# Second layer of a fused attention and mixture-of-experts kernel: biases of the sorted tiles summed by TensorE, row transfers held to planned steps, norms spread over more steps

## Time and profile before

| what | value |
|---|---|
| median of 3 runs | 2873.52 us (2866.96 to 2877.98) |
| profiled execution, its own time | 2869.59 us |
| its span | 2867.9 us |
| VectorE busy | 2243.4 us, 78% |
| ScalarE busy | 1236.5 us, 43% |
| TensorE matmuls busy | 1195.6 us, 42% |
| GpSimd busy | 289.9 us, 10% |
| first `B` of batches 0, 1, 2, 3 | 1572.9, 1798.4, 2093.3, 2416.2 us |
| last `B` of batch 3, end | 2694.6, 2867.9 us |

### The profile page before, as it was taken

How to read it: one execution, slowest core, us unless ns; L and a number is a source line. 1 busy time by engine, 2 the same in 40 slices (tenths; PEclk the granted TensorE clock), 3 DMA queues, 4 the chain that set the end, 5 groups by cost and what they waited for, 6 DMA issues and landing times. The chain is left out here.

```text
span 2867.9 us, 37860 instructions
## 1 busy us (share of the span) xinstructions
PE 1195.6 (42%) x7272; PEld 536.4 (19%) x7272; DVE 2243.4 (78%) x15187; ACT 1236.5 (43%) x3176; POOL 289.9 (10%) x425
## 2 busy tenths in 40 slices
PE   3010100101010000101004887788876887778697
PEld 1000000000000000000001111223421342133365
DVE  5999999999999999999975899856657665864133
ACT  1333333333333333333360556656655664567542
POOL 0000000000000000000010020031023212201211
PEclk9999999999999999999996899979987998889898
DMA  5000000000000000000034020103110212001100
GB/s 135 1 1 1 1 1 1 1 1 1 1 1 1 1 1 1 1 1 1 1 68 103 1 67 20 24 22 89 26 44 23 74 37 52 18 17 30 33 1 23
DMA packets 79603, 66.11 MB, mean 23 GB/s; under 512 B 8126, under 2 KB 64232, under 8 KB 79368
## 3 DMA queue, kind: packets, MB, share of 16 engines
q1 hardware_dynamic: 76296, 57.40, 8.3%
q0 software_dynamic: 3072, 6.30, 0.7%
HBM read 34.77 MB, written 28.57 MB: 22 GB/s over the span
## 5 line engine op out<-in xcount | busy, mean ns | idle before, releaser
L1309 DVE TENSOR_REDUCE nm_half<-pair 128x2 f32<-128x1024 f32 x512 | 611.7, 1219 | 224.1 <-PE pair L1557 188.6
L203 ACT ACTIVATE ex<-row,nmax 128x65 f32<-128x65 f32 x960 | 336.0, 350 | 923.8 <-DVE nmax L305 837.3
L1196 ACT ACTIVATE pt<-pair 128x1024 f32<-128x1024 f32 x512 | 510.2, 1027 | 389.2 <-PE pair L1567 357.9
L263 DVE SCALAR_TENSOR_TENSOR junk<-ex,tab 128x65 f32<-128x65 f32 x2850 | 620.0, 218 | 1.4 <-issue 0.4
L366 PE MATMUL p_s<-tab,bdg 128*128 128x32 f32 x120 | 31.9, 406 | 829.2 <-DVE tab L268 829.2
L1533 PE MATMUL p_o<-pt,va 128*9 128x512 f32 x2048 | 299.2, 659 | 9.7 <-ACT pt L1196 8.3
L268 DVE TENSOR_TENSOR tab<-raw,rz 128x1 f32<-128x1 f32 (+1 forms) x1890 | 284.8, 151 | 3.2 <-issue 1.1
L297 DVE SCALAR_TENSOR_TENSOR junk<-ex,rz,row 128x65 f32<-128x65 f32 x930 | 265.4, 285 | 3.0 <-issue 2.7
L1557 PE MATMUL pair<-ks,qs 48*128 48x512 bf16 x1024 | 212.8, 420 | 123.3 <-ACT pt L1196 75.4
L1567 PE MATMUL pair<-qs,ks 50*128 50x512 bf16 x1024 | 209.7, 414 | 62.4 <-DVE nm_half L1309 30.4
L263 DVE DVE_READ_ACCUMULATOR junk<-ex,tab 128x1 f32 x2850 | 233.8, 82 | 0.3
(11 more groups left out here) (254 smaller groups left out, 1908.1 us busy)
## 6 DMA issues: line engine op xcount, KB each, us to landing
parts_dram<-parts SPq DMA_DIRECT2D x48, 256.0 KB, 3.6
qs<-parts_dram SPq DMA_DIRECT2D x32, 192.0 KB, 4.8
ks<-parts_dram SPq DMA_DIRECT2D x32, 192.0 KB, 5.4
hid<-xs_dram SPq DMA_DIRECT2D x15, 256.0 KB, 2.9
ys_dram<-hid SPq DMA_DIRECT2D x15, 256.0 KB, 2.4
h_dram<-f SPq DMA_DIRECT2D x20, 128.0 KB, 2.5
x<-in_x SPq DMA_DIRECT2D x4, 512.0 KB, 8.4
w_W<-in_W SPq DMA_DIRECT2D x1, 2048.0 KB
```

Source lines behind the costliest of these rows:

```text
L203: nc.scalar.activation(ex[:, r % 2, :], row[:, r % 2, 1:], ACT.Exp, bias=nmax[:, r % 2:r % 2 + 1], accum_out=z[:, r % 2:r % 2 + 1]).then_i ...
L263: nc.vector.scalar_tensor_tensor(junk[:, g, :], ex[:, k, :], 1.0, tab[:, g, r:r + ROW], ALU.mult, ALU.mult, accum_out=raw[:, g:g + 1]).the ...
L1196: nc.scalar.activation(pt[:, kt % 2, :, tokens(t)], pair[fill.pair][:, :, :], ACT.Exp, scale=SCALE).then_inc(s_exp, 1)
L1309: nc.vector.reduce_max(nm_half[:, t, hp % 2, :, q], pair[fill.pair][:, :, :], AX.X, negate=True)\
```

## The change

- `RT` no longer builds `bias_t`: it compares the chosen expert with a column of numbers into `picked` (24 x 23, bf16), 1 where the row belongs to the tile's expert.
- The biases are split once into three bf16 parts, stacked in 24 rows (`b1_parts`), in a new step `BS` of the prologue: a load of 8 x 512 by SyncE, four operations of VectorE on 8 partitions, two small transfers to stack them. It stands behind the loads `ST` and ahead of the first maxima.
- `HS`: for each of the four chunks one bf16 product of 24 rows (`b1_parts` against `picked`, 256 columns for two tiles) starts the sum, and the float32 products of both tiles are added to it. ScalarE then does one Gelu of 128 x 4 x 256 without a bias, in place of eight.
- `SC` and `YG`: each step, not only the first, waits until the Exps of all units before its place in the plan are done. After batch 3 all eight `YG` wait for the last Exp.
- `SC` is due one a unit (14 to 21) instead of two a unit (15 to 18). `ADD` is due at 11 and 14 instead of 12 and 13. Norms 1 and 2 are due at 27 to 47 instead of 14 to 23. The groups stand at 29, 34, ... 54 instead of 26, 32, ... 56. The budget falls by 1.7 twice in a unit and by 3.0 in a unit of a group, and the due line rises faster after unit 48.

```diff
-         9: [("GA",), ("GE",)], 10: [("GB",)], 11: [("GC",)], 13: [("RK",)], 14: [("RT",)],
-         15: [("SC", 0), ("SC", 1)], 16: [("SC", 2), ("SC", 3)], 17: [("SC", 4), ("SC", 5), ("CT", 0)],
-         18: [("SC", 6), ("SC", 7), ("CT", 1)], 19: [("B2", 0), ("B2", 1)]}
-TAIL = {**{u: [("YG", u)] for u in range(QT)}, 8: [("XR",)], 12: [("ADD", 0)], 13: [("ADD", 1)], 14: [("LNS", 1, 0)],
-        15: [("LNS", 1, 1)], 16: [("LND", 1)], 17: [("LNN", 1, 0)], 18: [("LNN", 1, 1)], 19: [("LNS", 2, 0)],
-        20: [("LNS", 2, 1)], 21: [("LND", 2)], 22: [("LNN", 2, 0)], 23: [("LNN", 2, 1), ("OUT",)]}
-GROUP_AT = (26, 32, 38, 44, 50, 56)
+         9: [("GA",), ("GE",)], 10: [("GB",)], 11: [("GC",)], 13: [("RK",)],
+         14: [("RT",), ("SC", 0)], 15: [("SC", 1)], 16: [("SC", 2)],
+         17: [("SC", 3), ("CT", 0)], 18: [("SC", 4), ("CT", 1)], 19: [("SC", 5), ("B2", 0)], 20: [("SC", 6), ("B2", 1)],
+         21: [("SC", 7)]}
+TAIL = {**{u: [("YG", u)] for u in range(QT)}, 8: [("XR",)], 11: [("ADD", 0)], 14: [("ADD", 1)], 27: [("LNS", 1, 0)],
+        29: [("LNS", 1, 1)], 31: [("LND", 1)], 33: [("LNN", 1, 0)], 35: [("LNN", 1, 1)], 39: [("LNS", 2, 0)],
+        41: [("LNS", 2, 1)], 43: [("LND", 2)], 45: [("LNN", 2, 0)], 47: [("LNN", 2, 1), ("OUT",)]}
+GROUP_AT = (29, 34, 39, 44, 49, 54)
...
-    busy = [0.0]
+    busy, scored = [0.0], [2 * QT * HP * s]
...
-        least = 2 * u - 10 if moe else 5 * u // 2 + 1
+        least = 2 * u - 10 + max(0, u - 48) // 2 if moe else 5 * u // 2 + 1
...
+            if name in ("SC", "YG"):
+                x = *x, scored[0]
...
-        busy[0] = max(0.0, busy[0] - 1.9)
+        busy[0] = max(0.0, busy[0] - 1.7)
+        scored[0] = 2 * (QT * HP * s + u)
...
-            busy[0] = max(0.0, busy[0] - 5.0)
+            busy[0] = max(0.0, busy[0] - 3.0)
...
-            + [("ST", g, 1) for g in range(4)] + in_turn(0, FIRST_READY) + [("MN", 0), ("MT", 0)])
+            + [("ST", g, 1) for g in range(4)] + [("BS",)] + in_turn(0, FIRST_READY) + [("MN", 0), ("MT", 0)])
...
+                elif name == "BS":
+                    sp.dma_start(full[0:E, :], io["b1"]).then_inc(s_b1, 16)
+                    wait(s_cut, 4)
+                    for k in range(2):
+                        sp.dma_start(b1_parts[E * (k + 1):E * (k + 2), :], b1_sent[:, k, :]).then_inc(s_b1, 16)
...
+                    pool.wait_ge(s_exp, x[2])
                     for k in range(2):
                         i = QT * k + q
                         nc.gpsimd.indirect_dma_start(
...
-                    act.wait_ge(s_bias, s)
-                    act.sem_inc(s_pace_act, 1)
                     act.wait_ge(s_hs, 2 * NG * (s - 1) + x[1] + 1)
-                    for j in tiles:
-                        for f in range(FC):
-                            ins = nc.scalar.activation(hs[:, g % 2, f, tile(j % GROUP)], pair[fill.pair][:, j % 2, tile(f)],
-                                                       ACT.Gelu, bias=bias_t[:, j, f:f + 1])
-                    ins.then_inc(s_gs, 1)
+                    n, first = P * len(tiles), P * (tiles[0] % GROUP)
+                    nc.scalar.activation(hs[:, g % 2, :, first:first + n], by_chunk(pair[fill.pair])[:, :, 0:n],
+                                         ACT.Gelu).then_inc(s_gs, 1)
...
-                    then(nc.vector.tensor_tensor(before_t[:, :, :], expert_t[:, :].unsqueeze(2).broadcast_to((P, NT, E)), tiled,
-                                                 ALU.is_equal))
-                    then(nc.vector.tensor_tensor(bias_e[:, :, :, :], before_t[:, :, :].unsqueeze(2).broadcast_to((P, NT, FC, E)),
-                                                 cols[:, 4:4 + E * FC].rearrange("p (e f) -> p f e", f=FC).unsqueeze(1)
-                                                 .broadcast_to((P, NT, FC, E)), ALU.mult))
-                    nc.vector.reduce_sum(bias_t[:, :, :], bias_e[:, :, :, :], AX.X).then_inc(s_bias, 1)
+                    nc.vector.tensor_scalar(picked[:, :], expert_t[0:3 * E, :], parted[:, :], None, ALU.is_equal)\
+                        .then_inc(s_picked, 1)
+                elif name == "BS":
+                    b1, left = full[0:E, :], rest[0:E, :]
+                    dve.wait_ge(s_b1, 16)
+                    nc.vector.tensor_copy(b1_parts[0:E, :], b1).then_inc(s_cut, 1)
+                    dve.wait_ge(s_cut, 1)
+                    nc.vector.tensor_tensor(left, b1, b1_parts[0:E, :], ALU.subtract).then_inc(s_cut, 1)
+                    dve.wait_ge(s_cut, 2)
+                    nc.vector.tensor_copy(b1_sent[:, 0, :], left).then_inc(s_cut, 1)
+                    dve.wait_ge(s_cut, 3)
+                    nc.vector.tensor_tensor(b1_sent[:, 1, :], left, b1_sent[:, 0, :], ALU.subtract).then_inc(s_cut, 1)
...
-                    for j in tiles:
-                        for f in range(FC):
-                            ins = nc.tensor.matmul(pair[fill.pair][:, j % 2, tile(f)],
-                                                   w1[:, j % GROUP, tile(f)],
-                                                   xst[:, g % 2, tile(j % GROUP)], start=True, stop=True)
+                    to, n = by_chunk(pair[fill.pair]), len(tiles)
+                    for f in range(FC):
+                        nc.tensor.matmul(to[:, f, 0:P * n], b1_parts[:, tile(f)],
+                                         picked[:, tiles[0]:tiles[0] + n].unsqueeze(2).broadcast_to((3 * E, n, P)),
+                                         start=True, stop=False)
+                        for i, j in enumerate(tiles):
+                            ins = nc.tensor.matmul(to[:, f, tile(i)], w1[:, j % GROUP, tile(f)],
+                                                   xst[:, g % 2, tile(j % GROUP)], start=False, stop=i == n - 1)
```

52 lines of the change are left out of this document (34 added, 18 removed).

## The result

Forecast was 2848 us (2815 to 2888), faster. Measured: 2913.38 us, median of 4 runs (2907.66 to 2919.68), against 2872.01 us (2866.96 to 2877.98) for the kernel before. The ratio is 1.0144 with a 95% interval of 1.0115 to 1.0173: slower by some 41 us.

The account below looks back on a forecast made before the run. It took GpSimd's indirect-transfer stalls (56.2 us) as the largest reachable bound, beside VectorE, TensorE in groups and the prologue. Terms -28.2 + 5 + 5 - 6 - 6 + 5 = -25.2 us from 2869.6, plus 3.9 to the median: 2848 us, range 2815 to 2888.

Parts of the forecast that it names:

- held transfers: `SC` and `YG` steps in batches 1 to 3: d, what each of 40 steps still costs, is 0.4 us; -28.2 us.
- run after batch 3: The last 16 gathers start at the last Exp, so they and VectorE's wait end later; +5 us, bounds -4 and +6.
- `BS`: Prologue, ahead of VectorE's first maxima: issue 0.4, landing 2.5, four operations 2.8 us; taken +5, bounds 3.5 and 6.
- `RT`: VectorE in batches 1 to 3: loses two large and two smaller operations against one small; -6 us, bounds 0 and -8.
- norms: Units 16 to 23 gain 14.4 us by spreading, 8 come back later; -6 us, bounds -14 and +4.
- biases, one Gelu: 18 groups: eight bf16 products added to each, less ScalarE's 0.95 us; candidates 0, +6, +29, taken +5 us.
- budget, groups, due lines: The plan: same number of maxima, and groups every five units leave room for copies; 0 us, bounds -4 and +4.
- rival 3: `HS` in the groups: the switch of type costs 0.32 us a product, +29 in place of +5, 2872 us; chance 0.10.
- ScalarE's lateness: End of each group: ScalarE is 0.95 us behind TensorE, so that much of the eight products' cost is hidden.
- the unknown 2%: Chain share "another core or an unknown queue", some 57 us: stalls while GpSimd issues indirect transfers and TensorE's results arrive late.
- The sum of the stalls: Waits during GpSimd's runs of gathers and sendings: 44.2 us in the batches and 12.0 after them, 56.2 us.
- Rival 2: Held steps in batches 1 to 3: each pair hides results anew; at 2.0 us a step +39 us, 2912; chance 0.12.

Follow-up runs that it names:

- experiment 2: The bias part alone (`BS`, eight bf16 products a group, one Gelu, short `RT`) put into the kernel before: 2932.65 us, ratio 1.0186.
- experiment 5: The changed kernel with the four bias products of a pair of tiles ahead of its sixteen float32 instructions: 2860.53 us, ratio 0.9951.
- experiment 8: The changed kernel with TensorE's four register loads of expert numbers moved from a group's first `HS` to behind its `XS`: 2863.45 us, ratio 0.9959.
- experiment 9: The kernel before with only TensorE's register loads moved from a group's first `HS` to behind its `XS`: 2855.39 us, ratio 0.9947.
- experiment 6: The changed kernel with the load of `b1` issued right behind the prologue's first load of rows, not behind the sixteen `ST` loads: 2903.05 us, ratio 1.0090.
- experiment 12: The kernel before with the held transfers and groups at 28, 33, 38, 44, 50, 56, so the first rows load two units later: 2816.74 us, ratio 0.9837.
- experiment 1: The kernel before with the held transfers alone, `SC` due one a unit: 2842.37 us, ratio 0.9880.

## Why the prediction was wrong

By its own terms:

| term | predicted | what the runs showed |
|---|---|---|
| held transfers | -28.2 (d = 0.4) | -34 alone, -47 with room for the rows |
| run after batch 3 | +5 | -4.1 after the last `B` |
| `BS` | +5 | +14.0 (first maximum 16.4 later, 2.4 of it older than the step); 0 when loaded early |
| `RT` | -6 | -6.7 in units 16 to 23 of experiment 2 |
| norms | -6 | -23 |
| biases, one Gelu | +5 | +53 alone less `BS` and `RT`: some +45; +67 in all in the changed kernel |
| budget, groups, due lines | 0 | batch 0 +10.3; the plan as a whole +15, the norms' gain within it |

**The step that failed** is the price of the bias products in a group: "Taken +5, near the middle one, since that row has both the type and the place". It had three things wrong.

The size: the three prices were 0.13, 0.16 and 0.32 us; measured 0.36 us at full clock. The trace of before did show a bf16 product between float32 ones, the 0.32 us of an `A`. I scaled it by its columns. Experiment 5 shows why that was wrong: in a run of four the products start 0.11 us apart, so the columns are cheap, and the edges are the price. That was rival 3 with its 0.32 us, though it laid the price on the type. The Trainium skill (TensorE: Matmul & The Clock Gate, section "Back-to-back issue gap") led to 109 ns; the run of four in experiment 5 agrees, with 0.108 to 0.112 us from start to start, and the interleaved order costs three times as much.

The 0.95 us a group that ScalarE's lateness was to hide: it does not show in most groups. Six groups with eight bias products ran at full clock both in the kernel before and in experiment 2. Unit 38 of batch 2 and units 32, 44 and 50 of batch 3 grew by 2.4, 3.0, 3.3 and 3.1 us, where 8 x 0.36 = 2.9 would be the whole price. Only the first groups of batches 1 and 2, with no `YS` in them, grew by less, 1.4 and 1.1 us.

The clock, which had no term: the groups stood at its lower level for 31 us before, 82 in experiment 2 and 91 in the change (from each group's length and mean clock), and half of what was added is lost, 26 to 30 us. With some 51 us for the products themselves (1.43 for each of 33 pairs of tiles, 1.24 for three single tiles) that makes 77 to 81; the groups grew by 69 (experiment 2) and 79. The prediction named as a sign of being wrong a group that grows by over 1 us; they grew by 4.4 on average.

**What I did not look at** was the wait ahead of `HS`. It was in the trace of before (1.4 to 2.2 us in most groups), ScalarE was named as the late one, and the four register loads behind it were in no view that counts busy time. A longer `HS` at a fallen clock costs twice its length, and the fall itself was there in 9 groups of the kernel before. In experiments 8 and 9, which took the wait away, 10 and 9 falls of 18 became one each. By the Trainium skill (DMA: Bandwidth & Descriptors, section "Latency and other measured facts") `tensor_load` has a floor of about 600 ns; here a single load took 0.30 us, less than that, and from the start of one to the next it was 0.66 us. Beside the transfers of `PO` a load took 0.9 to 1.2 us.

**`BS`.** The working of the four operations was right (0.41 + 0.68 + 0.41 + 0.68, in 2.2 us where 2.8 was allowed). The landing was taken from transfers elsewhere, 2.5 us; this one stood behind sixteen loads on the same queue and took 11.8 us, and experiment 6, which put it ahead of them, took the loss away. Even the bounds, 3.5 to 6, did not hold it.

**Budget at 0.** The same number of maxima, yes, but put off in batch 0, whose end then waits for them, and in unit 63 of batch 2 (14.2 us, with nine maxima in a row).

**The end.** +5 became -4.1. The run did start later, but the wait behind it did not move with it: it fell to 3.21 us. Why is not shown.

**What was right.** That the unknown 2% were GpSimd's runs of indirect transfers, that holding them lets TensorE's results through, `RT`, the Gelu (1.02 us), units 16 to 23 under 45 us, and the sign of the norms. The sum of the stalls, 56.2 us, was a little high: the chain has 49.6, chiefly since 4.0 us of the second sending are "issue" in the earlier trace rows and 4.6 of ScalarE's 6.05 in the first are on the chain. That the transfers would stand in pairs was wrong (runs of up to eight), and the hold worked all the same. Its cost was near what was chosen: in experiment 12 units 1 to 15 of batches 2 and 3 grew by 5.8 and 3.8 us, 0.6 us for each of the sixteen steps of gathers, where d was 0.4. The rule of the Trainium skill that was weighed (SBUF — State Buffer, section "Who interferes with whom", by which the gain is nil) did not decide: experiments 1 and 12 took 34 and 47 us away by holding those transfers. Whether it is a contention of memory at all, or only that TensorE's signals are late, no run here tells. Rival 2 named the right time, 2912, by luck: its price, 2 us in each of 40 steps, was not paid. The lower end of the range, 2815, is no sum of the terms named for it, which give 2822.

## What to carry to other kernels

Price an added instruction in its place in the engine's stream, at the edges to its neighbours, and not by its own size; if its weights have far fewer rows than theirs, put its like together. Before adding work to a stretch that one engine fills without a gap, look at what the stretch waits for at its start, register loads too, and at the granted clock behind that wait. A small load costs the queue ahead of it: issue it before the large ones, even if it is wanted last.

## What was not expected of the hardware

- Between a product with 24 rows of weights and one with 128 TensorE lost about 0.1 us at the edge, and a float32 product behind it as much again: starts lie 0.112 us apart inside a float32 run, 0.208 and then 0.213 behind a bias product; 3.46 against 2.58 us for the same 20 instructions in two orders. The same delays stand between float32 products of 8 and of 128 rows (0.200 and 0.213), so a change of type is not needed for them; between 50 and 48 rows there is none.
- TensorE's clock fell to half inside a stretch of full work after waits that seem short: in the change in 9 of the 12 groups ahead of which TensorE had stood for 1.78 us or more, and in one of the six with 1.24 us or less. Where it had stood for 0.9 us or less ahead of all 18 (experiment 8) it fell in one, the same group.
- Four register loads took 2.2 us, and 5.2 us beside the twelve transfers of `PO`.
- TensorE's results reached other engines 6 us late and more during runs of sixteen indirect transfers, 2 to 3 us late in or behind some runs of six or eight, and behind runs of two or four no late one was found (traces of the change and of experiments 1 and 12).
